# A pre-norm decoder layer on one core: Gelu evaluated twice on ScalarE in place of a cast on VectorE, one maxima tile for each head pair of the cross attention, two residual buffers in place of a copy, and new orders of the steps

## What is computed

```python
x = x + attn(_layernorm(x))          # softmax(q k^T / 16) v, projections with biases
x = x + xattn(_layernorm(x), ctx)    # softmax(q k^T / 4) v over 77 context tokens, mask
x = x + ffn(_layernorm(x))

def ffn(x):
    xn, se = rms_norm(x, gamma_x), rms_norm(slot_embeds, gamma_slot)
    logits = einsum('bsd,etd->bset', xn, se)
    dispatch = softmax(logits, axis=1)                  # over the tokens
    slots = einsum('bsd,bset->betd', xn, dispatch)
    processed = gelu(slots @ w1, approximate=False) @ w2
    combine = softmax(logits.reshape(b, s, e * t), axis=-1)
    return einsum('bnd,bsn->bsd', processed, combine)
```

## Time and profile before

| what | value |
|---|---|
| median of 3 runs | 1714.13 us (1713.97 to 1718.77) |
| the profiled execution's own time | 1718.86 us |
| its span in the trace | 1717.1 us |
| PE, DVE, ACT, POOL busy | 1633.2, 1287.0, 979.1, 540.1 us |
| share of the span | 95%, 75%, 57%, 31% |
| mean granted TensorE clock | 0.989 of full speed |
| DMA over the span | 19.48 MB, mean 11 GB/s |

### The profile page before, as it was taken

The page is one execution under the profiler, slowest core; times in us unless marked ns, Lnnn a source line. Parts: engine busy times, 40 slices in busy tenths (PEclk is TensorE's granted clock), DMA queues, the critical chain, the costliest instruction groups (busy, mean ns, idle before and its releaser), DMA issues.

```text
span 1717.1 us, 37771 instructions
## 1 busy us (share of the span) xinstructions
PE 1633.2 (95%) x15552; PEld 1475.2 (86%) x15552; DVE 1287.0 (75%) x2778; ACT 979.1 (57%) x1505; POOL 540.1 (31%) x450
## 2 busy tenths in 40 slices
...
DMA packets 20843, 19.48 MB, mean 11 GB/s; under 512 B 9920, under 2 KB 19776, under 8 KB 20288
## 3 DMA queue, kind: packets, MB, share of 16 engines
...
...
## 4 chain that ended last, share of the span: by engine, by line
PE 79%; DVE 9%; ACT 8%; issue 3%; POOL 1%; DMA 0%; DVEq 0%; SPq 0%; ACTq 0%
PE ps L453 20%; PE ps L454 18%; PE ps L455 18%; PE ps L574 3%; DVE mx L1122 2%; PE ps L561 2%; ACT pt L879 2%; PE ps L541 2%; PE ps L731 2%; PE ps L650 2%; PE ps L585 2%; PE ps L662 2%; PE ps L495 1%; ACT L959 1%; ACT h_f L959 1%
## 5 line engine op out<-in xcount | busy, mean ns | idle before, releaser
L1456 POOL TENSOR_TENSOR h_lo<-h_f,h_hi 128x512 fp32r<-128x512 f32 x256 | 336.3, 1321 | 462.0 <-DVE h_hi L1332 462.0
L453 PE MATMUL ps<-sl_hi,w_hi 128*128 128x256 f32 x1024 | 302.5, 295 | 6.0 <-DVE sl_lo L1014 3.8
L453 PE MATMUL ps<-w_hi,h_hi 128*128 128x256 f32 x1024 | 299.5, 292 | 7.5 <-POOL h_lo L1456 7.5
L454 PE MATMUL ps<-sl_hi,w_lo 128*128 128x256 f32 x1024 | 289.9, 283 | 0.0
L455 PE MATMUL ps<-sl_lo,w_hi 128*128 128x256 f32 x1024 | 289.9, 283 | 0.0
L454 PE MATMUL ps<-w_hi,h_lo 128*128 128x256 f32 x1024 | 289.7, 283 | 0.0
L455 PE MATMUL ps<-w_lo,h_hi 128*128 128x256 f32 x1024 | 289.6, 283 | 0.0
L453 PEld LDWEIGHTS ps<-sl_hi,w_hi 128*128 128x128 f32 x1024 | 196.1, 192 | 32.5 <-issue 16.5
L453 PEld LDWEIGHTS ps<-w_hi,h_hi 128*128 128x128 f32 x1024 | 196.1, 191 | 19.9 <-POOL h_lo L1456 18.3
L959 ACT ACTIVATE h_f<-ps 128x512 f32<-128x512 f32 x256 | 150.6, 596 | 104.6 <-PE ps L455 103.9
L1462 POOL TENSOR_TENSOR cb_lo<-ecomb,cb_hi 128x512 fp32r<-128x512 f32 x60 | 82.0, 1367 | 381.9 <-ACT ecomb L974 381.9
...
## 6 DMA issues: line engine op xcount, KB each, us to landing
...
```

What stands on the lines that cost most here:

```text
L453: te.matmul(o, lhs[0], rhs[0], start=first, stop=False)
L454: te.matmul(o, lhs[1], rhs[0], start=False, stop=False)
L1456: Q_.tensor_tensor(h_lo[:, part, :], h_f[:, part, :], h_hi[:, part, :].bitcast(f32), ALU.subtract)\
```

## The change

It has four parts and a fifth that follows from them.

1. **Gelu twice.** `ge` issues two ACTIVATE on the same bank: one writes `h_hi`, which is rounded to fp32r as it is written, the other `h_f`. VectorE's `hid` is gone, and with it the signal `h_hi`; GpSimd's `hid` waits for `ge`.
2. **One maxima tile.** In `md2` the maxima of even heads are in column 16 and those of odd heads in column 0 of the same 32; `mt2` has two transposes. `sh2` holds both groups now; a new GpSimd step `qm` writes q2 times the 0/1 column into it (two instructions), and `sh2` on VectorE adds the transposed maxima times the other column.
3. **Two buffers.** `x2` is `x2_even` or `x2_odd` by the batch; `keep` and `res` are gone.
4. **Norms by group.** In `START` `nrm` and `nrm2` can be called for one group (`first_nrm`): shuffle, reciprocal and product for it alone, so that the first group's norm comes before the last group's results.
5. **New orders** of all four engines. `START` has 246 idle matmuls in place of 152.

```diff
             def mt2(a, c):
...
-                for e in range(2):
-                    for t in range(NT):
-                        last = te.transpose(ps[:, 0, e * S + t * P:e * S + (t + 1) * P],
-                                            md2[:, t, e, :, :].rearrange("p i w -> p (i w)"), ident[:, :])
+                for t in range(NT):
+                    last = te.transpose(ps[:, 0, t * P:(t + 1) * P], md2[:, t, :, :].rearrange("p i w -> p (i w)"),
+                                        ident[:, :])
...
             def ge(b, c, q):
...
+                nc.scalar.activation(h_hi[:, 2 * q:2 * q + 2, :], halves(hidden_bank(b, q)), ACT.Gelu)
                 nc.scalar.activation(h_f[:, 2 * q:2 * q + 2, :], halves(hidden_bank(b, q)), ACT.Gelu).then_inc(s["ge"], 1)
...
+            def first_nrm(a, c):
+
+                step = "rl" if c else "la"
+                dve.wait_ge(s["ml"], nth("ml", a, 2 * c + 1))
+                V.stream_shuffle(od[:, c, :], lsum[:, c, :], [8 * c + HD * (1 - r // HD) for r in range(2 * HD)])\
+                    .then_inc(s["ls"], 1)
+                dve.wait_ge(s["ls"], nth("ls", a, c + 1))
+                V.reciprocal(od[:, c, :], od[:, c, :]).then_inc(s[step], 1)
+                dve.wait_ge(s[step], nth(step, a, 1))
+                dve.wait_ge(s["ml"], nth("ml", a, 2 * c + 2))
+                last = V.tensor_tensor(od[:, c, :], xo[:, c, :], od[:, c, :], ALU.mult)
+                if c:
+                    last.then_inc(s["od"], 1)
...
             def sh2_step(a, c):
...
+                dve.wait_ge(s["q2_m"], nth("q2_m", a, 1))
                 for e in range(2):
-                    last = V.scalar_tensor_tensor(sh2[:, e, :], q2[:, c, :], half[:, e:e + 1],
-                                                  ps[:, 0, e * S:(e + 1) * S], ALU.mult, ALU.add)
+                    last = V.scalar_tensor_tensor(sh2[:, c, e, :], ps[:, 0, 0:S], half[:, 1 - e:2 - e],
+                                                  sh2[:, c, e, :], ALU.mult, ALU.add)
...
-            def keep(b):
-
-                dve.wait_ge(s["x2"], nth("x2", b, 1))
-                if later(b):
-                    dve.wait_ge(s["y"], nth("y", b - 1, 1))
-                V.tensor_copy(res[:, :, :], x2[:, :, :]).then_inc(s["res"], 1)
...
-            def hid(b, c, q):
-                n = 4 * c + q
-                dve.wait_ge(s["ge"], nth("ge", b, n + 1))
-                V.tensor_copy(h_hi[:, 2 * q:2 * q + 2, :], h_f[:, 2 * q:2 * q + 2, :]).then_inc(s["h_hi"], 1)
...
+            def qm(a):
+                pool.wait_ge(s["q2_sb"], nth("q2_sb", a, 1))
+                if later(a):
+                    pool.wait_ge(s["st2_ps"], nth("st2_ps", a - 1, C))
+                for e in range(2):
+                    last = Q_.tensor_scalar(sh2[:, :, e, :], q2[:, :, :], half[:, e:e + 1], None, ALU.mult)
+                last.then_inc(s["q2_m"], 1)
+
             def hid(b, c, q):
-                pool.wait_ge(s["h_hi"], nth("h_hi", b, 4 * c + q + 1))
+                pool.wait_ge(s["ge"], nth("ge", b, 4 * c + q + 1))
```

One line of the PE table of `ORDER`, before and now:

```diff
-        m.slots.2 m.outer.1.1 c.mt.1 m.hidden.2.0 c.shifted.1 m.hidden.2.1 c.scores.2 c.pv.1 m.hidden.2.2 m.hidden.2.3
+        m.slots.2 m.outer.1.1 c.mt.1 c.shifted.1 m.hidden.2.0 m.hidden.2.1 c.scores.2 c.pv.1 m.hidden.2.2 m.hidden.2.3
```

More of the change, by code:

```diff
@@ L88 @@
-        d0.mt2.0 d0.shifted2.0 c1.q d0.scores2.1 d0.pv2.0 c1.v d0.mt2.1 s1.idle.3 d0.shifted2.1 s1.idle.6 s1.idle.2
-        c1.scores.0 d0.pv2.1 s1.idle.6 s1.idle.4 s1.idle.1 c1.mt.0 s1.idle.1 c1.shifted.0 s1.idle.4 s1.idle.3
-        s1.idle.1 c1.scores.1 d0.oproj2 s1.idle.3 s1.idle.2 c1.pv.0 s1.idle.2 s1.idle.2 c1.mt.1 s1.idle.1 c1.shifted.1
-        d0.xt.3 d0.logits.0 d0.logits.1 d0.logits.2 d0.logits.3 m0.dispatch.0 c1.scores.2 c1.pv.1 m0.slots.0 c1.mt.2
-        c1.shifted.2 m0.hidden.0.0 m0.hidden.0.1 m0.rxt c1.scores.3 c1.pv.2 m0.hidden.0.2 m0.rmb m0.hidden.0.3 c1.mt.3
@@ L98 @@
-        m0.slots.3 c2.scores.3 d1.oproj2 m0.outer.2.1 c2.mt.3 c2.pv.2 c2.shifted.3 d1.xt.3 m0.hidden.3.0 m0.hidden.3.1
-        m0.hidden.3.2 c2.pv.3 d1.logits.0 m0.hidden.3.3 d1.logits.1 m0.combine.2 c2.oproj d1.logits.2 d1.logits.3
+        s0.idle.12 c0.xt.1 s0.idle.13 c0.k c0.q s0.idle.2 c0.v s0.idle.25 c0.scores.0 s0.idle.12 c0.mt.0 s0.idle.2
+        c0.shifted.0 s0.idle.8 c0.scores.1 c0.pv.0 s0.idle.12 c0.mt.1 s0.idle.2 c0.shifted.1 s0.idle.8 c0.scores.2
+        s0.se_transp.0.0 c0.pv.1 s0.idle.9 c0.mt.2 s0.idle.10 c0.shifted.2 s0.idle.8 c0.scores.3 c0.pv.2
@@ new lines @@
+        s0.se_transp.0.1 s0.idle.6 c0.mt.3 s0.idle.2 c0.shifted.3 s0.idle.8 c0.pv.3 s0.se_transp.1.0 s0.idle.13
+        c0.oproj s0.se_transp.1.1 s0.idle.1 d0.kv s0.idle.10 d0.xt.2 s0.idle.6 d0.q2 s0.idle.4 c1.xt.1 d0.scores2.0
+        s0.idle.2 c1.k d0.mt2.0 c1.q d0.shifted2.0 s0.idle.9 d0.scores2.1 d0.pv2.0 s0.idle.8 d0.mt2.1 c1.v
+        d0.shifted2.1 c1.scores.0 d0.pv2.1 s1.idle.11 c1.mt.0 s1.idle.2 c1.shifted.0 s1.idle.7 d0.oproj2 c1.scores.1
+        c1.pv.0 s1.idle.7 c1.mt.1 s1.idle.4 c1.shifted.1 s1.idle.6 d0.xt.3 s1.idle.6 d0.logits.0 d0.logits.1
@@ new lines @@
+        d0.logits.2 d0.logits.3 m0.dispatch.0 c1.scores.2 c1.pv.1 m0.slots.0 s1.idle.7 c1.mt.2 s1.idle.2 c1.shifted.2
+        m0.hidden.0.0 m0.hidden.0.1 c1.scores.3 c1.pv.2 m0.hidden.0.2 m0.rxt m0.hidden.0.3 c1.mt.3 s1.idle.2 m0.rmb
+        c1.shifted.3 d1.kv m0.outer.0.0 c1.pv.3 m0.dispatch.1 m0.outer.0.1 c1.oproj m0.slots.1 m0.hidden.1.0
+        m0.hidden.1.1 c2.xt.1 c2.k c2.q c2.v m0.hidden.1.2 m0.hidden.1.3 m0.combine.0 d1.xt.2 c2.scores.0 d1.q2
+        c2.mt.0 c2.shifted.0 m0.outer.1.0 d1.scores2.0 c2.pv.0 m0.dispatch.2 d1.mt2.0 d1.shifted2.0 m0.slots.2
@@ L100 @@
+        m0.outer.1.1 m0.hidden.2.0 d1.scores2.1 d1.pv2.0 m0.hidden.2.1 m0.hidden.2.2 d1.mt2.1 d1.shifted2.1
+        m0.combine.1 c2.scores.1 d1.pv2.1 m0.hidden.2.3 c2.mt.1 m0.dispatch.3 c2.shifted.1 m0.outer.2.0 c2.scores.2
+        c2.pv.1 m0.slots.3 c2.mt.2 c2.shifted.2 d1.oproj2 c2.scores.3 m0.outer.2.1 c2.mt.3 c2.pv.2 c2.shifted.3
+        m0.hidden.3.0 d1.xt.3 m0.hidden.3.1 c2.pv.3 d1.logits.0 d1.logits.1 m0.hidden.3.2 m0.hidden.3.3 m0.combine.2
+        c2.oproj d1.logits.2 d1.logits.3
     """,
@@ L110 @@
+        c2.ex.3 d1.xt.3 m0.ge.3.0 m0.pr.2 m0.ge.3.1 d1.logits.0 m0.ge.3.2 m0.ge.3.3 d1.logits.1 d1.logits.2
         d1.logits.3
@@ L132 @@
+        m0.hid.3.0 m0.hid.3.1 m0.hid.3.2 m0.hid.3.3
     """,
```

205 lines of the change are left out of this document (101 added, 104 removed).

## The result

The changed kernel takes **1707.38 us** (median of 5 runs, 1706.85 to 1708.17); the kernel before, run beside it, 1717.31 (5 runs, 1713.97 to 1718.77). The ratio is 0.9945, with a 95% interval of 0.9934 to 0.9956: faster by half a per cent. The forecast was 1701.5 with 1690 to 1718 as its range: the direction and the range hold.

A forecast was written before the change was run, and what follows sets the result against it. PE's work and waits bound the iterations, latency chains and the clock START and FINISH. Transposes -6.1, moved line 0, second Gelu +1.3 and +1.3, START -7.3, FINISH -1.8 make -12.6 from 1714.13: 1701.5 us, range 1690 to 1718.

The forecast's parts named there:

- The moved line: Iterations: shifted scores right behind the second pair's maxima transposes; 13 more `qz` waits, +6.8, against `pt` and `h_f` waits, -6.8.
- Gelu twice, +2.6: Chunk 0 of each iteration: the second Gelu makes `h_lo` late, +1.3 us, and an Exp behind it late, +1.3 us.
- The new product: GpSimd's product ahead of the second `h_lo`, taken as 1.3 us each: 0, at worst 21 us in all.
- (b): START, norms by group in the self and cross attention of batch 0: +1.6 us together.
- (a): START, clock: idle matmuls leave PE no long pause, five stretches up to the logits get shorter, -8.4 us.
- (d): START: `mt2.1` no longer stands behind the queries' shuffles, -0.8 us.
- (c): START: batch 1's `mx.1` moves from beside `oproj2` to between `x2` and its statistics, +2.3 us.
- (e): START from 122.6 to 245.4 us: VectorE loses 16 casts, -2 us, between -8 and +4.
- the norms and the pauses eat START's gain: Rival, chance 0.20: idle matmuls are fixed work and delay PE where waits are shorter than planned; START's gain goes, 1711 us.
- the stretches at 1.2 GHz may only move: Rival, chance 0.06: START's clock does not come back, so its -8.4 us goes; 1710 us.
- FINISH, -1.8: FINISH: `oproj2` fills one of the weight load's four waits for `h_lo`, -1.8 us, between -5 and +1.
- `h_lo` late in every chunk: Rival, chance 0.14: at `outer.c.0`, 0.5 us late in each of four chunks, 26 us in all, 1727 us.

The follow-up runs named there:

- the run of the old line: The changed kernel with the third chunk's first hidden product back between the second head pair's maxima transposes and its shifted scores in the iterations: 1716.57 us, ratio 1.0003.

## Why the prediction was right and wrong

The forecast's gain of 12.6 us and the 10.7 between the profiled spans (9.9 by the medians) are close in part by luck. With the transposes shared out (4, 26 and 2 steps) it had -8.1 for START, -2.3 for the iterations and -2.2 for FINISH; measured were -0.6, -5.6 and -4.5. START was overrated by 7.5 and the two others underrated by 5.6 together.

- **Transposes, -6.1.** Right: 0.17 a step measured, 0.19 counted; some 5.5 us.
- **The moved line, 0.** Wrong, 8 us in the run. The exchange named was the one that took place (39 waits for `qz`, none for `pt` or `h_f`), but its wait for `h_f` was priced at 0.2, as in the earlier trace rows, from a kernel in which the second Gelu does not stand ahead of it. Terms of one sum were priced each against the old kernel, though one changed the price of the other.
- **Gelu twice, +2.6.** Wrong as a cost of its own: 25 us alone, in the old orders. With the new orders nothing of it is seen as a wait of PE's matmuls, only as 0.4 us of its weight load. The forecast's "equal, where both engines are free" did not help there, since ScalarE is not free everywhere: in the chunk shown above it goes from `sl_hi` to the Gelus without a gap. In an iteration this term and the one above were missed with opposite signs: 99.97 us before, 0.34 less by the transposes, is 99.63; 99.49 was measured. All else nets to -0.14, where the forecast had +0.2 (2.6 over 13). What belongs to the Gelus and what to the orders in this is not told apart.
- **The new product, 0 between 0.7 and 2.2 each.** The size was 1.57, and the 0 held, with `h_lo` ending 0.05 us ahead of its use. The 2.7 us of spare time that the forecast gave GpSimd were not there beyond the product itself: doubling it cost all of its 3.1 us, and as much again by a second stop and the clock.
- **START, -7.3: mis-sized by the most.** It went 0.6 us down in the profiled executions, and by the medians its new orders are worth 3 us. Stretch by stretch (before, after) the traces show where:
  - Up to `shifted.1` +1.2 (35.55, 36.75), which no term had. It is no more than executions with the same orders differ by: ten of them have that step at 35.2 to 36.8.
  - (b) The norm ahead of `shifted.2` +2.0, and from `pv.3` to `oproj` -1.0: both as counted.
  - (a) From `oproj` to `shifted2.0` 23.9 us became 17.2, -6.8, where four terms of (a) had -6.7; the logits themselves -1.5, where it had -1.7. The clock's price was right, and 5.5 us of it come off with the 36 idle steps of one run.
  - **The step that failed:** from `shifted2.0` to `oproj2` 21.6 us became 24.2, +2.7, where (b) and (d) together had -0.2. The sum gave the half clock back and had no term for a new stretch of it: `pv2.1` and 22 idle matmuls took 5.9 us in place of 3.8. `shifted2.1` came 1.1 us later besides, with the first group's norm ahead of it.
  - (c) From `oproj2` to the logits +1.5, where the forecast had +2.3. Undone alone, (c) and the norms change nothing in the whole time.
  - (e) The part behind the logits was counted at -2 and measured +1.3 (122.9, 124.2), but 121.5 in the run of the old line with the same orders: what it is worth stays open.

  Of the rivals, "the norms and the pauses eat START's gain" is what happened in these two executions, and in small "the stretches at 1.2 GHz may only move" as well.
- **FINISH, -1.8.** 4.5 was measured by the windows, 0.3 of it the two steps of transposes. The forecast had counted only the out-projection. PE's waits for `h_lo` there fell from 7.5 to 3.4 us, but two new ones came, 2.2 for `od` by that very out-projection and 1.9 for `edt`. What belongs to the casts and what to the orders was not taken apart.
- **What the rivals said of chunk 0.** `h_lo` late in every chunk did not happen, but the runs with the product doubled or alone show that its mechanism was one step away, and its price too low (26 us, against 84 and 53).
- **The signs named in advance.** `qz` 39 times and `pt` none, PEclk 0.97, 64 records at the transposes: as said. An iteration is 99.49, just below the 99.6 to 100.0 named. The logits 6 us earlier: wrong, 0.4. ScalarE 1096 us against 1107, VectorE 1185 against 1138, which has no bearing on the time.

Still open: what decides where START's stretches at the half clock fall and how long START is with them, and what in the orders of the iterations gives ScalarE's results their time (only the moved line was undone). Whether GpSimd's new product delays instructions of VectorE, as the forecast's passage on the cast's 416 to 1115 ns feared, was not looked at.
